# A two-block graph network on one core: edges counted in one packed product, block 1 fed with centred x, and the last tile normalised by two engines

## What is computed

```python
def gat_conv(x, src, dst, W, a_src, a_dst, b, heads, out_ch):
    h = (x @ W).reshape(n, heads, out_ch)
    alpha_src = einsum('nhc,hc->nh', h, a_src)
    alpha_dst = einsum('nhc,hc->nh', h, a_dst)
    e = leaky_relu(alpha_src[src] + alpha_dst[dst], 0.2)
    m = segment_max(e, dst)
    p = exp(e - m[dst])
    alpha = p / segment_sum(p, dst)[dst]
    return segment_sum(h[src] * alpha[:, :, None], dst) + b

# block 0
h = elu(gat_conv(x, src, dst, W1, ..., 8, 768))
x1 = _layernorm(x + gat_conv(h, src, dst, W2, ..., 1, 768))
# block 1
h = gat_conv(x1, ..., W1, 4, 256)
h = relu(layer_norm(h, g1, be1)) + (x1 @ Wr1 + br1)
h2 = layer_norm(gat_conv(h, ..., W2, 1, 768), g2, be2)
out = _layernorm(x1 + h2 + (h @ Wr2 + br2))
```

## Time and profile before

| | us |
|---|---|
| median of three runs | 373.2 (372.81 to 374.55) |
| profiled execution | 373.22 |
| its span | 371.1 |
| TensorE busy | 355.4 (96% of the span) |
| GpSimd busy | 247.6 |
| Vector busy | 219.4 |
| ScalarE busy | 213.7 |

### The profile page before, as it was taken

How to read it: one execution, slowest core, us unless ns; L and a number is a source line. 1 busy time by engine, 2 the same in 40 slices (tenths; PEclk the granted TensorE clock), 3 DMA queues, 4 the chain that set the end, 5 groups by cost and what they waited for, 6 DMA issues and landing times.

```text
span 371.1 us, 6198 instructions
## 1 busy us (share of the span) xinstructions
PE 355.4 (96%) x2104; PEld 304.1 (82%) x2104; DVE 219.4 (59%) x570; ACT 213.7 (58%) x373; POOL 247.6 (67%) x170
## 2 busy tenths in 40 slices
PE   7899979999999999999999999998988999999994
PEld 4788868888988988898898898897666788888883
DVE  3996766428328345543741923736776788763875
ACT  4996466756755664673765665565352667244601
POOL 2789619595866947849668595692268976397911
PEclk9999999999999999999999999999999999999999
DMA  7979936637637536754663752755073256436002
GB/s 250 320 244 262 389 128 197 224 95 250 178 96 257 184 134 180 241 172 126 215 239 98 251 174 91 241 188 204 0 219 134 90 165 193 165 94 242 8 0 85
DMA packets 24544, 65.15 MB, mean 176 GB/s; under 512 B 1952, under 2 KB 3024, under 8 KB 24528
## 3 DMA queue, kind: packets, MB, share of 16 engines
q1 hardware_dynamic: 20720, 55.19, 44.7%
q10 hardware_dynamic: 3808, 9.76, 8.8%
HBM read 64.15 MB, written 0.79 MB: 175 GB/s over the span
## 4 chain that ended last, share of the span: by engine, by line
PE 71%; ACT 7%; DVE 6%; issue 6%; POOL 5%; DMA 4%; SPq 0%; POOLq 0%; DVEq 0%; ACTq 0%
PE ps L918 52%; PE ps L1202 7%; PE ps L1003 6%; DMA raw<-in_L_gnn_W 4%; POOL ring_lo L364 3%; ACT ring_hi L351 2%; PE ps L982 1%; PE ps L1268 1%; PE ps L1036 1%; ACT rows_hc L689 1%; POOL ring_lo L380 1%; ACT z L689 1%; PE ps L968 1%; ACT am L689 1%; POOL x_sb L619 1%
## 5 line engine op out<-in xcount | busy, mean ns | idle before, releaser
L364 POOL TENSOR_TENSOR ring_lo<-raw,ring_hi 128x768 fp32r<-128x768 f32 x94 | 170.7, 1851 | 75.1 <-ACT ring_hi L351 75.0
L351 ACT ACTIVATE ring_hi<-raw 128x768 fp32r<-128x768 f32 x96 | 77.5, 851 | 35.2 <-PE ps L918 28.6
L380 POOL TENSOR_TENSOR ring_lo<-raw,ring_hi 128x512 fp32r<-128x512 f32 (+1 forms) x40 | 59.7, 1521 | 24.0 <-ACT ring_hi L373 23.9
L1402 DVE CUSTOM_DVE_ANT_0 e<-ps,att 128x768 f32<-128x768 f32 (+1 forms) x54 | 40.0, 796 | 51.3 <-PE ps L918 48.7
L918 PE MATMUL ps<-ring_hi,zT_hi 128*128 128x512 f32 (+1 forms) x256 | 69.4, 346 | 0.9 <-DVE zT_lo L1558 0.6
L918 PE MATMUL ps<-ring_lo,zT_hi 128*128 128x512 f32 (+1 forms) x256 | 67.4, 338 | 0.0
L918 PE MATMUL ps<-ring_hi,zT_lo 128*128 128x512 f32 (+1 forms) x256 | 67.2, 338 | 0.0
L918 PE MATMUL ps<-ring_hi,xT_hi 128*128 128x512 f32 x192 | 51.3, 343 | 2.3 <-POOL ring_lo L364 1.0
L918 PE MATMUL ps<-ring_lo,xT_hi 128*128 128x512 f32 x192 | 50.3, 339 | 0.0
L918 PE MATMUL ps<-ring_hi,xT_lo 128*128 128x512 f32 x192 | 50.2, 338 | 0.0
L918 PEld LDWEIGHTS ps<-ring_hi,zT_lo 128*128 128x128 f32 x256 | 43.2, 188 | 5.6
(11 more groups left out here) (163 smaller groups left out, 562.2 us busy)
## 6 DMA issues: line engine op xcount, KB each, us to landing
raw<-in_L_gnn_W SPq DMA_DIRECT2D x54, 768.0 KB, 4.4
raw<-in_L_gnn_Wr SPq DMA_DIRECT2D x8, 768.0 KB, 4.3
att<-in_L_gnn_a_src ACTq DMA_DIRECT2D x10, 384.0 KB, 4.6
att<-in_L_gnn_a_dst ACTq DMA_DIRECT2D x10, 384.0 KB, 5.4
raw<-in_L_gnn_W SPq DMA_DIRECT2D x4, 384.0 KB, 6.1
x_sb<-in_x SPq DMA_DIRECT2D x3, 256.0 KB, 5.7
rows_hc<-in_L_gnn_b SPq DMA_DIRECT2D x1, 512.0 KB, 6.3
rows_hc<-in_L_gnn_g SPq DMA_DIRECT2D x1, 512.0 KB, 7.2
```

The lines of the kernel that those rows point to most:

```text
L351: eng.activation(slot_hi(c), raw_chunk(c), ACT.Copy).then_inc(hi_done, 1)
L364: eng.tensor_tensor(slot_lo(c), raw_chunk(c), slot_hi(c).bitcast(F32), ALU.subtract)\
L380: eng.tensor_tensor(ring_lo[:, q["ring_at"]:q["ring_at"] + w], raw[:, q["raw_group"], q["raw_at"]:q["raw_at"] + w], ring_hi[:, q["ring_at" ...
L1402: dve.tensor_tensor_reduce(junk[:, at:at + w], of[:, (k - first_head(a)) * w:(k - first_head(a) + 1) * w], att[:, half_at * row + k * w:ha ...
```

## The change

**Counting.** One one-hot of 128 columns a group, with the value -1 for a destination in the lower half and 4096 in the upper one, and `steps` (ScalarE's Sign, or a comparison on Vector) in place of ramps: one matmul of 257 columns a group. The first difference along the columns holds both halves' counts in one number; Vector takes them apart by adding and subtracting a large constant, and adds the loops from `ident`. ScalarE copies the counts. `scores(0)` comes before counting. The edges are loaded from SP's queue, b1 later on ScalarE's. Vector makes the low parts of four chunks of the first phase, not two.

**Softmax.** ScalarE computes `leaks` (0.2 x the score), Vector takes the maximum with the score itself (`leaky_scores`), masks by a minimum (`tile_tops`), and ScalarE does one exponential where it did two.

**Block 1.** The transposes and products use x - mean; 1/sqrt(var) is applied later: as a factor in the feature copies and dot products, by ScalarE on x itself (`x1_scale`), and on the residual's product (`residual_scale`), with `residual_bias` behind it.

**The end.** Vector and ScalarE each normalise one half of tile 1, and each half has its own queue.

```diff
-FIRST = 2
+FIRST = 4
...
+            sp.dma_start(edges[:, 0, :], src.rearrange("(p t) -> p t", p=P)).then_inc(edges_loaded, 16)
+            sp.dma_start(edges[:, 1, :], dst.rearrange("(p t) -> p t", p=P)).then_inc(edges_loaded, 16)
...
-            def ramps(first, end):
+            def steps(first, end):
                 for t in range(first, end):
-                    bias = edges_f[:, 0, t:t + 1] if t < ET else self_f[:, t - ET:t - ET + 1]
-                    act.activation(ramp(t), iota[:, :], ACT.Relu, bias=bias).then_inc(ramp_act_done, 1)
+                    act.activation(step(t), iota[:, :], ACT.Sign, bias=src_bias[:, t:t + 1]).then_inc(step_act_done, 1)
...
+            def leaks(a):
...
+                for i in range(NT):
+                    act.wait_ge(a_dst_done, before(a) + heads_of(a) * (i + 1))
+                    for k in range(heads_of(a)):
+                        at = s_at(a, k)
+                        act.activation(e1[:, first_head(a) + k, i, :], ps[:, at:at + N], ACT.Identity,
+                                       bias=a_d[:, pair(a, k, i)], scale=SLOPE).then_inc(leak_done, 1)
...
-                        act.activation(e1[:, k, i, :], at, ACT.Exp, bias=bias1[:, c:c + 1]).then_inc(e_done, 1)
-                        act.activation(at, at, ACT.Exp, bias=bias2[:, c:c + 1], scale=SLOPE).then_inc(e_done, 1)
+                        act.activation(at, at, ACT.Exp, bias=top[:, pair(a, k, i)], scale=-1.0).then_inc(e_done, 1)
...
+            leaks(0)
             att_for(1)
-
-            act.wait_ge(counted, NT)
-            act.activation(ramp_sum, ps[:, COUNT_AT[0]:COUNT_AT[0] + NT * N], ACT.Copy).then_inc(ramps_copied, 1)
-            for c in (0, 1, 2):
+            for c in (0, 1):
                 split_hi(act, 2, c)
+            act.wait_ge(counted, 1)
+            act.activation(step_sums, ps[:, STEPS_AT:STEPS_AT + 1 + N], ACT.Copy).then_inc(sums_copied, 1)
...
+            chunks_hi(3, 6)
+            centre_wide(0)
+            chunks_hi(6, 7)
+            x1_hi(0)
+            centre_wide(1)
+            chunks_hi(7, 9)
+            x1_hi(1)
+            x1_scale(0)
+
             features_hi(A_GAT1A, tiles=(0,))
             chunks_hi(9, 14)
+            x1_scale(1)
             features_hi(A_GAT1A, tiles=(1,))
...
+            act.activation(x_sb[:, 1, cols], y[1][:, cols], ACT.Copy, scale=rstd[:, 1:2]).then_inc(act_normed, 1)
+            act.wait_ge(act_normed, len(ON_ACT) + 1)
+            act.dma_start(out[P:N, cols], x_sb[:, 1, cols]).then_inc(stored, 16)
...
+                    last = pe.matmul(ps[:, STEPS_AT:STEPS_AT + 1 + N], hot(t), step(t), start=t == 0, stop=t == ET - 1)
...
+            pe.wait_ge(z_hi_done, 1)
+            for c in (0, 1):
+                chunk(2, c)
+                first_accumulate(c, 1, passes=FIRST_TWO)
             pe.wait_ge(z_lo_done, 1)
             clear_acc(0)
...
             def transpose_x1(i):
 
-                pe.wait_ge(x1_done, i + 1)
+                pe.wait_ge(wide_centred, i + 1)
...
+                    if i == 0 and q["k"] == 5:
+                        residual_bias(0, 0)
+                        residual_bias(0, 1)
...
+                for i in range(NT):
+                    for k in range(n):
+                        at = s_at(a, k)
+                        dve.tensor_tensor(masked_at(a, k, i), ps[:, at:at + N], e1[:, first_head(a) + k, i, :], ALU.max)\
+                           .then_inc(leaky_done, 1)
...
+                    dve.tensor_tensor_reduce(at, at, far[:, i, :], -1.0, 3.0e38, ALU.add, ALU.min, top[:, pair(a, k, i)])\
+                       .then_inc(masked, 1)
...
+            dve.tensor_scalar(in_upper, packed, PACK - 1.5, ROUND, ALU.add, ALU.add).then_inc(rounded, 1)
+            dve.wait_ge(rounded, 1)
+            dve.tensor_scalar(in_upper, in_upper, ROUND, 0.0, ALU.subtract, ALU.max).then_inc(unpacked, 1)
+            dve.wait_ge(unpacked, 1)
+            dve.tensor_tensor(in_lower, in_upper, packed, ALU.subtract).then_inc(unpacked, 1)
...
             y_piece(0, 0)
             y_piece(0, 1)
-            y_stats(0)
+            y_centre(0)
             y_piece(1, 0)
-            x1(0)
             y_piece(1, 1)
-            y_stats(1)
+            y_centre(1)
             x1_lo(0, 0)
             x1_lo(0, 1)
-            x1(1)
+            y_stats(0)
+            y_stats(1)
             x1_lo(1, 0)
             x1_lo(1, 1)
```

## The result

The changed kernel takes **377.9 us** (median of four runs, 377.7 to 378.2) against 373.3 before (372.8 to 374.6): a ratio of 1.0134, 95% interval 1.0115 to 1.0154. The prediction was 369.9 and a range up to 372.9, so the forecast had the wrong sign and the range doesn't hold the result. The profiled execution took 378.18 us with a span of 376.4, 5.3 more than before.

What follows compares the result with a forecast made beforehand. TensorE, with 71% of the chain, was taken to bound the kernel. Opening and ELU chains -4.4, block 1's start with its stall +1.8, its rest -0.3 and tail -0.4 gave -3.3: 369.9 us, range 366.9 to 372.9.

Steps and rivals of the forecast that it cites:

- Opening, TensorE's side: Opening: 32 counting matmuls instead of 66 save 3.6 us, a shorter wait 0.9; head 0's weight transposes could start at 37.4.
- Opening, ScalarE's side: Opening: ScalarE's copy of the step sums, then Vector's chain, come last; head 0's transposes start at 38.2, 3.7 us earlier.
- ELU chains: Heads 0 and 1: a dot product moved into Vector's wait gains 0.7 us; head 1's 0.8 longer softmax is absorbed.
- Heads 2 to 7: Block 0's steady heads: normalised weights still come in time with 0.6 us of slack, so nothing changes.
- Rival (3): Steady heads: each softmax is late from more engine crossings; 375.3 us at 1.5 us extra latency; chance 0.08.
- Conv2 and block 1's start: Second convolution to block 1: leaks cost 0.25 us, centring without waiting for statistics puts TensorE 3.55 ahead.
- The wait at chunk 9: Block 1's start: TensorE waits 4.4 us for GpSimd's low part of chunk 9, behind the shifts of x1.
- Rival (1): Block 1's new wait: the clock falls to half, costing 0.5 to 1.4 us; 371.0 us in all; chance 0.22.
- The two small waits: Block 1: two TensorE waits of about 0.6 us behind the chunk 9 wait.
- Block 1, the rest: Block 1 later: bias matmuls move into the products, 0.3 us off; leaks and exponentials of both half layers fit.
- End: Tail: ScalarE takes one half with its own queue, both stores go together, 0.4 us off; its subtraction runs during GpSimd's power.
- the stall: Block 1's wait for GpSimd's low parts: 5.35 us lost without the clock, chunk 11 starting 1.8 later than before.

Runs made afterwards that it cites:

- e1: Changed kernel with one-hots from number 4 on, not 12, reading column numbers from PSUM instead of SBUF: 371.9 us, ratio 0.9961.
- e6: Changed kernel with all 32 one-hots, not 12, reading the bf16 column numbers in SBUF: 386.3 us, ratio 1.0332.
- e7: Changed kernel with 20 matmuls of zeros in TensorE's opening wait before the scores of head 0: 377.2 us.
- e8: e3 with the old softmax for every head but head 0, row maxima in SBUF and a wrong sign in the destination term: 376.2 us.
- e9: e3 with Vector writing the centred half of the last tile to PSUM, not SBUF, at the end: 368.5 us.
- e10: e8 with the row maxima in PSUM and the sign of the destination term corrected: 366.6 us, ratio 0.981.
- e3: Changed kernel with both repairs, the one-hot edit of e1 and the late shifts of e2: 368.0 us, ratio 0.988.
- e5: e3 with head 0's scores behind counting, ScalarE copying the step sums first and Vector unpacking counts ahead of low parts: 368.2 us.
- e2: Changed kernel with GpSimd's row sum behind chunk 20 and its x1 shifts between the hidden layer norm's inverse roots: 374.7 us, ratio 1.0045.
- e11: e3 with the end of the kernel before, both halves on Vector and both stores on SyncE: 368.1 us.

## Why the prediction was wrong, step by step

**Opening, TensorE's side: the step that failed.** It counts the 32 matmuls right, and says of Vector that it has low parts, six small edge operations and six step rows earlier in its queue. It says nothing of the 32 one-hots on Vector, now half as wide: it put them at nothing, without a reason. Eight of them cost 8.2 us, not 2.6. The sum had -3.7 for the opening, the trace has +3.85; e1 takes 6.9 of the 7.55 us between them away with one constant, and e6 makes it worse with the same one. Of these 6.9, 1.95 are the half clock behind TensorE's wait (e7). Without this fault (e1) the change takes 371.9 against the 369.9 forecast; the other 2.0 lie in the terms below.

The rows shown ahead of the prediction had this mechanism, and I used it in the wrong place. The earlier trace rows has Vector's scaling of tile 1 at 1.63 us beside GpSimd's low parts. The same operation for tile 0, with GpSimd at rest, in the kernel before:

```profile
277.00 0.68 DVE L1666 TENSOR_SCALAR x_sb<-z,mv,rstd 128x768 f32<-128x768 f32 x1 [1.16 <-POOL rstd L632]
```

I put 0.3 us on it (GpSimd's chunks at 1.27, not 1.36), and never asked which operations the change newly puts beside GpSimd. The diff shows it, in a line that my excerpt left out: twelve one-hots read `iota` (bf16, SBUF), where the kernel before read `iota_ps` for all. The Trainium skill (SBUF — State Buffer, "Who interferes with whom") states this rule: Vector and GpSimd share a port pair; a form of Vector that uses two ports takes it, and so does one with two SBUF inputs where GpSimd reads SBUF; whoever comes second waits for the whole instruction. The traces agree: 1887 ns for a one-hot of 305, 1.71 us for two columns of 0.16 (e8), 0.42 for GpSimd's 0.19, and none of it where one side is in PSUM (e1, e9, e10). That it is the port and not another shared thing is the Trainium skill's statement; the runs show that it takes GpSimd at work (e6) and that the place of the operands decides.

**Opening, ScalarE's side: right in the number, the path only half.** With the one-hots mended, head 0's weights start at 38.85 and 39.06 (38.2 forecast), and ScalarE copies the sums at 32.2 and 32.4 without a wait (31.2 forecast). But "this now comes last" is a tie: Vector's low parts and leaky maxima, which the sum doesn't have, end at 32.95 in e3, just when the copy is there, and the copy 3.5 us earlier gains 0.3 (e5). That the number held is in part luck.

**ELU chains: right in the sum.** From head 0's weights to head 2's scores the lag falls by 1.02 (3.85 to 2.83), 0.7 forecast. The longer softmax of head 1 shows as a wait of 0.7 in the changed kernel, absorbed in the next position as argued.

**Heads 2 to 7: right.** TensorE has no wait at their weights; it gained 0.5 over the six. Rival (3), the slower side I named, did not happen: what made the kernel slower stood on no list.

**Conv2 and block 1's start: right, but the clock.** Forecast -3.55, measured -3.07 to the scores of the first half layer (+2.37 to -0.70); the leaks cost 0.5 there, not 0.25. The wait at chunk 9: 4.4 forecast, 4.25 measured, for the reason given (e2). **Rival (1) came true with it, at a smaller price**: the clock fell, and cost TensorE 1.3 us of matmul time in this execution and 2.4 in e1's. Most of the 1.3 is hidden, as the rival itself said in part: by GpSimd's row the low part of chunk 11, the third of its five, ends at about 298.1, and TensorE starts chunk 11 at 298.39. So the path lost some 0.3 (an estimate from these two rows), less than the rival's 0.5 to 1.4, and 1.1 more in e1, where the half clock went on behind chunk 11. I had left the clock out of the sum since the row allowed both. The rule of the Trainium skill weighed there (TensorE: Matmul & The Clock Gate, Part 1) was right in both waits of over 4 us, after which the granted clock is 0.50, and should have had the forecast's place. Lost at this place: 5.55 of lag (4.89 between the scores and the weights, and 0.66 of bias matmuls that now come later), 5.35 forecast without the clock. The two small waits that I expected behind the first did not occur: at the half clock three matmuls take 1.28, and GpSimd makes a chunk in 1.24.

**Block 1, the rest: sizes off.** The bias matmuls gave 0 of the 0.3: the lag with them in it is 4.85 at the first half layer's weights and 4.99 at the last aggregation. "Leaks and exponentials of both half layers fit" held only because TensorE stood still; with the stall gone they are late by 1.9 (e2), and 1.1 of it remains even with the old softmax (e10).

**End: the wrong sign.** -0.4 forecast, +0.3 measured. GpSimd's addition, held by Vector's subtraction, cost 0.23; I had called the subtraction free because it "runs during GpSimd's power". The split itself gave 0.27 back: the last store is issued 2.08 us after the start of the last statistics, 2.12 before. And the span ended 2.6 us after that issue, in all traces with the last store on ScalarE's queue, where it is 2.3 and 2.4 after SyncE's second one (before, e11). Why the last part is longer stays open.

**The sum, term by term** (opening, ELU chains, heads 2 to 7, start of block 1, the stall, the rest of block 1, end). Forecast: -3.7 - 0.7 + 0 - 3.55 + 5.35 - 0.3 - 0.4 = -3.3. Measured in the traces: +3.85 - 1.02 - 0.46 - 3.07 + 5.55 + 0.14 + 0.31 = +5.3. All but 1.05 of the 8.6 us between them is the first term.

What stays open besides: why e10's first half layer still waits 1.10, which of Vector's scaled dot products and low parts is responsible. It wasn't tried. Nor was b1's load put back in front: TensorE waits 0.4 to 2.0 us for it in the traces since the change, and what of that reaches the end wasn't separated.

## What to carry to other kernels

List, for every operation that a change adds or moves on Vector or GpSimd, where its operands are and what the other engine does at that time; with both sides in SBUF a one-hot of 0.31 us or two columns of 0.16 waited for the end of GpSimd's operation, up to 1.9 us. Moving one operand to PSUM ended it here, at a small price: 0.33 us a one-hot in e1 where an undisturbed one of SBUF takes 0.25 (0.98 for four), 0.62 for the subtraction of 0.42 (e9). A row whose duration is double that of its twin is a mechanism, not a number to correct by. And when a change makes TensorE earlier, look for what its slowness covered: here GpSimd's written-out queue and two softmaxes took most of the gain in block 1, and the repair was to move work that nobody waited for.

## What the runs showed of the hardware that I had not expected

An operation of two columns on Vector took 1.71 us beside GpSimd (e8), and one of a single column on GpSimd 0.42 in place of 0.19 beside Vector: size is no protection. Beside GpSimd one one-hot gets through for each of its operations (four of 1874 to 1996 ns in a row beside four low parts in e2), and GpSimd isn't slowed: four low parts take 7.27 us in the changed kernel and 7.29 in e1. So the 28 one-hots of e6 cost 0.79 each on average against 0.32 in e1, and what counts is how many operations of GpSimd they meet. And the same wait of 4.2 us was followed by 2.7 us at the half clock in the changed kernel's trace and by 3.5, 4.9 and 5.3 in those of e6, e7 and e1. The price of such a stall differs by a microsecond; whether by kernel or by execution these single traces don't tell.
